# Who issues the rows of maxima: ScalarE's queue in place of SyncE's in two attention stages

## The reference

```
h = concatenate([x, latents], axis=1)                 # 256 + 256 tokens
q = (latents @ q_w + q_b).reshape(b, 256, 16, 16)     # 16 heads of width 16
kmat, v = the two halves of (h @ kv_w + kv_b)         # 512 keys
attn = einsum('bkhd,bnhd->bhkn', q, kmat) / 16
attn = where(full_mask, attn, -inf)
attn = softmax(attn)                                  # over the 512 keys
out = einsum('bhkn,bnhd->bkhd', attn, v) @ out_w + out_b + residual
out = rmsnorm(out); out = gelu(out @ mlp_w1 + mlp_b1) @ mlp_w2 + mlp_b2 + residual
```

## Time and profile before

| what | value |
|---|---|
| times, three runs | 1387.09, 1380.42, 1385.77 us, median 1385.77 |
| profiled execution | 1387.44 us, span 1385.6 us |
| PE busy | 1224.4 us (88%) |
| DVE busy | 991.2 us (72%) |
| ACT busy | 724.4 us (52%) |
| POOL busy | 496.1 us (36%) |
| granted clock of PE, mean over the span | 0.932 |
| DMA, mean over the span | 51 GB/s |
| exponential of a shifted score, line 1849 | 256 times, mean 605 ns, 132.1 us busy |
| row maxima, line 1864 | 128 times, mean 1211 ns, 151.9 us busy |
| two layers' rows of maxima, line 1827 | 64 DMAs of 2 KB |

### The profile page before, as it was taken

How to read it: one execution, slowest core, us unless ns; L and a number is a source line. 1 busy time by engine, 2 the same in 40 slices (tenths; PEclk the granted TensorE clock), 3 DMA queues, 4 the chain that set the end, 5 groups by cost and what they waited for, 6 DMA issues and landing times. The chain is left out here.

```text
span 1385.6 us, 27506 instructions
## 1 busy us (share of the span) xinstructions
PE 1224.4 (88%) x9162; PEld 1010.4 (73%) x9162; DVE 991.2 (72%) x2232; ACT 724.4 (52%) x1644; POOL 496.1 (36%) x649
## 2 busy tenths in 40 slices
PE   4799999999599999999599699969599976599969
PEld 4699999999599999998588455559377756455558
DVE  5688778887588887887773689465488866589464
ACT  3466656666366665666542177541166642177441
POOL 2754555444274445542150000030199950000030
PEclk8899999999899999999899789979799998699979
DMA  4111111010210111010013875020660014874020
GB/s 151 47 31 32 32 30 30 23 30 0 95 37 26 31 31 30 10 36 0 31 65 56 133 82 61 13 77 1 190 138 2 2 51 86 108 83 55 13 65 31
DMA packets 56609, 70.91 MB, mean 51 GB/s; under 512 B 7340, under 2 KB 49118, under 8 KB 54178
## 3 DMA queue, kind: packets, MB, share of 16 engines
q1 hardware_dynamic: 55420, 66.40, 22.7%
q10 hardware_dynamic: 1086, 3.20, 0.9%
HBM read 46.79 MB, written 8.13 MB: 40 GB/s over the span
## 5 line engine op out<-in xcount | busy, mean ns | idle before, releaser
L804 ACT ACTIVATE a_prob<-a_s_ps,a_negmax 128x257 f32<-128x257 f32 x256 | 119.2, 476 | 92.3 <-DVE a_negmax L894 92.3
L1864 DVE TENSOR_REDUCE s_mx<-s_s_ps 128x2 f32<-128x1024 f32 x128 | 151.9, 1211 | 17.8 <-PE s_s_ps L1909 17.6
L1849 ACT ACTIVATE s_probT<-s_st_ps 128x512 f32<-128x512 f32 x256 | 132.1, 605 | 59.9 <-PE s_st_ps L1923 57.5
L743 POOL TENSOR_TENSOR x_v_hi<-a_v_sum,x_one 128x512 fp32r<-128x512 f32 x60 | 63.2, 1054 | 242.5 <-DVE a_v_sum L883 242.4
L368 POOL MEMSET r_power<- 128x8 f32 x3 | 0.3, 105 | 362.7 <-POOLq L1976 329.3
L1653 POOL TENSOR_SCALAR s_below<-s_masked,s_mx 128x256 f32<-128x256 f32 x256 | 118.6, 485 | 27.9 <-DVE s_mx L1681 27.8
L909 DVE TENSOR_TENSOR a_pT_lo<-a_t_ps,a_pT_hi 128x512 fp32r<-128x512 f32 x128 | 88.2, 689 | 35.9 <-ACT a_pT_hi L817 34.2
L894 DVE TENSOR_REDUCE a_negmax<-a_s_ps 128x2 f32<-128x514 f32 x128 | 86.9, 688 | 26.0 <-PE a_s_ps L951 24.2
L1681 DVE CUSTOM_DVE_ANT_0 s_masked<-s_s_ps,l_mask 128x256 f32<-128x256 f32 x256 | 90.7, 421 | 15.5 <-PE s_s_ps L1718 15.5
L817 ACT ACTIVATE a_pT_hi<-a_t_ps 128x512 fp32r<-128x512 f32 x128 | 76.7, 600 | 47.3 <-PE a_t_ps L1005 44.1
L1666 ACT ACTIVATE s_probT<-s_st_ps 128x512 f32<-128x512 f32 x128 | 69.7, 595 | 28.3 <-PE s_st_ps L1728 28.3
(11 more groups left out here) (272 smaller groups left out, 4068.4 us busy)
## 6 DMA issues: line engine op xcount, KB each, us to landing
x_wqk_raw<-L_xattn_wq SPq DMA_DIRECT2D x32, 128.0 KB, 2.3
x_wqk_raw<-L_xattn_wk SPq DMA_DIRECT2D x32, 128.0 KB, 2.2
x_wv_raw<-L_xattn_wv SPq DMA_DIRECT2D x16, 256.0 KB, 3.1
a_wo_raw<-L_xattn_wo SPq DMA_DIRECT2D x16, 256.0 KB, 3.1
l_k_st<-k_second SPq DMA_DIRECT2D x12, 256.0 KB, 9.0
l_k_st<-k_stack SPq DMA_DIRECT2D x16, 192.0 KB
l_q_st<-q_stack SPq DMA_DIRECT2D x12, 192.0 KB
x_vbias<-L_xattn_bias_v SPq DMA_DIRECT2D x2, 1024.0 KB, 4.7
```

The costliest lines, as they stand in the source:

```text
L804: nc.scalar.activation(prob[:, n % 2, qt, 0:NK], s_ps[:, n % 2, qt, 0:NK], ACT.Exp, bias=negmax[:, n % 2, qt:qt + 1], accum_out=den[:, n % ...
L1849: nc.scalar.activation(probT[:, third % 2, n // 4, n // 2 % 2, n % 2], st_ps[:, u % 3], ACT.Exp, scale=c.scale).then_inc(z.exp_done, 1)
L1864: nc.vector.tensor_reduce(mx[:, i % 2, qt, a::2], s_ps[:, n % 2], AX.X, ALU.max).then_inc(z.max_done, 1)
```

## The change

The two row DMAs leave SP's stream and go to ACT's. ACT's order of a round gets a new step R0 between the third exponential (E2) and the fourth (E3); in it ACT waits for `mx_out` of the `second` quad and issues the two DMAs on its own queue. PE's, DVE's and POOL's streams stay as they were. SP's stream keeps all its loads, with no wait between those of different rounds but the one of line 1837.

```
-    act_steps = steps("E0 E1 E2 E3 E4 O0 E5 E6 E7")
+    act_steps = steps("E0 E1 E2 R0 E3 E4 O0 E5 E6 E7")
...
                 def body(first, second, third, fourth):
-                    if second is not None:
-                        g, b = batch(second)
-                        sp.wait_ge(z.mx_out, second + 1)
-                        for half in range(2):
-                            m = half * HALF + c.MAX_ROW
-                            sp.dma_start(slots[g % 3][0][m:m + 1, :, b].bitcast(F32),
-                                         mxT[2 * half:2 * half + 2, second % 2].bitcast(F32)
-                                         ).then_inc(row_in[second % 2], 16)
                     if first in (0, 1):
                         second_unit.load(c, sp, first == 0, slots[1][first == 0], unit_in[0])
...
+                        elif kind == "R" and second is not None:
+                            g, b = batch(second)
+                            act.wait_ge(z.mx_out, second + 1)
+                            for half in range(2):
+                                m = half * HALF + c.MAX_ROW
+                                act.dma_start(slots[g % 3][0][m:m + 1, :, b].bitcast(F32),
+                                              mxT[2 * half:2 * half + 2, second % 2].bitcast(F32)
+                                              ).then_inc(row_in[second % 2], 16)
```

## The result

The changed kernel takes 1417.91 us (median of 4 runs, 1416.81 to 1424.55) against 1386.19 us (4 runs): a ratio of 1.0247, 95% interval 1.0222 to 1.0272 (a ratio is worked out from all runs, not from the two medians, whose quotient is 1.0229). The forecast was 1381.8 us, its range 1374 to 1394. The profiled executions have spans of 1415.0 and 1385.6 us, so the traces show 29.4 us of it. The mean granted clock of TensorE is 0.922 after and 0.932 before.

A forecast was written before the change was run, and what follows sets the result against it. The start was taken to wait for data, the rest as a closed loop of the engines. Terms -9.1 + 2.0 + 0.7 + 1.6 + 0.8 = -4.0 us took 1385.8 to 1381.8 us, range 1374 to 1394.

The forecast's parts named there:

- Part 1: First row of each stage, layers 2 and 4: in its own queue it lands earlier, -9.1 us in all.
- one packet of the loads on the same engine: First row's landing: one 8.2 KB load packet gets in the way on a DMA engine, adding 1.0 us.
- 1.60 us: Estimated time from a row's issue to PE's release, taken from the second row with q1 nearly drained.
- Part 4: Traffic SP now sends at once: full-clock row waits +1.6 us, ACT's issues while SP issues +0.8 us.
- Part 2: Second row of each stage, issued while loads fill the engines: one packet more per layer, +2.0 us in all.
- Part 3: ACT's steady round: the issue pair's 1.02 us delay fits the 1.03 us slack; jitter costs +0.7 us.
- the table load: Exponential's table load, moved behind the first DMA pair: has 3.4 us before the first exponential, cost 0.
- rows at full clock: Part 4's row waits beside SP's loads: 0.2 us in each of 8 rounds, +1.6 us.
- issue beside SP: Part 4's cost of ACT issuing while SP issues: 0.1 us in each of 8 rounds, +0.8 us.
- Rival A: R0 at full clock beside group 3's loads: ACT pays for SP's traffic, +11 to +22 us, around 1400; chance 0.19.
- threshold of 1.85: Rival A's limit: an ACT issue pair above 1.85 us makes the change a loss.
- Rival B: Row late whichever queue, engines full: Parts 1 and 2 fall to 0, +3.1 us, 1388.9 us; chance 0.14.

The follow-up runs named there:

- c_kq: a_behind with group 1's key and query loads sent at once and only later loads paced, rows on ACT: 1397.95 us, ratio 1.008 to the kernel before.
- b_sp_last: Kernel before, rows still on SP but issued behind the loads of the round instead of ahead of them: 1395.88 us, ratio 1.0078.
- a_behind: Changed kernel with SP pacing its loads: round 1 waits for the first row's landing, later rounds for ACT's fourth exponential: 1390.19 us, ratio 1.0028.
- f_four: a_behind with four row DMAs of 1 KB per quad instead of two of 2 KB: 1439.46 us, ratio 1.0393 to the kernel before.
- a_mx: Changed kernel with SP again waiting for the same maxima ahead of the loads, rows still on ACT: 1387.53 us, ratio 1.0033 to the kernel before.
- d: Kernel before, rows on SP, loads spread: three key loads each in rounds 0 and 1, query loads in round 2, group 2 a round later: 1388.07 us, ratio 1.0019.
- h: Loads spread as in g, but on a_behind's ACT rows and SP waits: 1380.91 us, ratio 0.9985 to the kernel before.
- i: g with the constant rows behind the loads of round 2 instead of in round 0: 1385.06 us, ratio 0.9997 to the kernel before.
- g: Kernel before, rows on SP, loads spread finely over rounds 0 to 6, constant rows in round 0: 1379.42 us, ratio 0.9955; repeated 1378.18 us, 0.9951.
- j: g with all six query loads in round 2 and the constant rows in round 3 behind the loads: 1375.0 us, ratio 0.9935 to the kernel before.

## Why the prediction was wrong

**The bound.** It was read rightly: the start waits for data, the steady round is a closed loop with 1.03 us of slack for ACT. All but some 0.7 us of the loss falls in the start. One reading was too strict, that "a delay of O0 lengthens the round by as much": in the changed kernel rounds of 6.10 and 6.22 us in layer 2 are each followed by one of 5.7, so a single delay of 0.2 to 0.3 us is made good.

**Part 1 is the step that failed:** "After the change the row has a queue of its own", with a landing of "one packet of the loads on the same engine" behind its 1.60 us. Summed at -9.1 us, it came out at (9.94 - 4.92) + (11.17 - 5.76) = +10.4. Two things were wrong in it. The queue counts for little when the DMA engines have a backlog: c_kq and b_sp_last, and before and a_behind, agree within 0.9 us in both layers. And the backlog was taken as it stood before, 1.57 MB, when the change itself raises it to 2.56 (in layer 4 2.7). Even my end for the bad case, "a row that lands behind all 1.57 MB as before gives 0", held the bytes fixed. The wait for the maxima on SP was a wait for the row's data, but it was also what spaced the loads; I wrote down in Part 4 that SP "is never held by maxima any more", and did not bring that to Part 1.

**Part 2** counts one packet for the second row too: +2.0 us, measured 7.0 in layer 2 and 10.95 in layer 4, some 18, for the same reason with 4.3 and 4.7 MB ahead. So the two waits are 28 of the 29.4 us.

**Part 3** is right in its mechanism: +0.7 us forecast. From the first copy out to the thirteenth, layer 2 takes 70.79 us, before 70.68, and layer 4's 0.74 us more are the late row at 1275.80. The period is 5.90 us, the pair 1.17 us, the idle time ahead of the copy out nil. f_four shows the edge beside which the change stands. That the table load is hidden is right too: 1.28 us at 786.39, PE's first E at 798.

**Part 4** had the traffic in view but the wrong place for its price. "That the loads arrive earlier gains nothing" is true, and missed that they cost. Its rows at full clock (+1.6 us) met only the loads of group 3, since those of group 2 were all through by 814 us; one of them was late, by 0.66 us in layer 4. The issue beside SP (+0.8 us) cost PE 1.6 us once in layer 2 and 0.6 in layer 4 (a pair of 1.95 us at 1228.18), both at the low clock.

**Rival A** did not decide: pairs of 1.47 to 1.60 us beside the loads of group 3 (835.20 above) lengthen single rounds by 0.2 us (831.64 to 837.74, 6.10), which the next round gives back, and stay below its threshold of 1.85. Its mechanism is there, though, and where it bit hardest was the low clock: single issues of up to 2.41 us at 800.59 while SP's took 2.16 and 2.35.

**Rival B** had the right reason, "the row is late anyhow, because the engines are full, whichever queue it is in", a chance of 0.14, and a price of +3.1 us. That is about what a_mx (ratio 1.0033) and a_behind (1.0028) measure: B describes a change that keeps SP's pace. The real one needed a fourth case, B with the bytes that the removed wait lets through: (2.56 - 1.57) MB at 131 GB/s are 7.6 us at the first row, and (4.33 - 2.36) MB 15.0 us up to the second. Measured in layer 2 were 5.3 (798.08 against 792.78) and 15.2 (813.37 against 798.13). The first figure is too high, as in the table above. Two layers at 15 us are +30, a time near 1416 us. This is worked out afterwards, but the bytes and the rate were in front of me, and Part 4 itself had SP through with all these loads by about 800 us.

**The two rules** that I weighed. The Trainium skill, DMA: Bandwidth & Descriptors, "Issuing engines are not separate DMA queues", says that a second issuing engine saves only sequencer time. The measured delay agrees: the second issuer bought the row 0.2 to 0.9 us. The section also says that the DMAs of several engines interleave, which this row, behind a backlog, did not show. The other section, "Queues, rings and completion order", says that an engine goes round its queues packet by packet; by it four packets of ACT's queue should have moved soon after 786, and none moved before 795. The measurement decides: with this backlog the row kept the order of issue, to within 0.3 MB.

**Open:** where that order is kept. Bytes that an engine has already taken up, or one list for both queues in front of the engines, would look the same in these traces; packets in flight are seen when they move, not when they are taken. The rows that found little ahead of them fit either. No run issues the rows from a third engine, or from ACT with the loads on yet another queue. Nor is the loss of a_mx and a_behind wholly split. Counted from the first key load, their first copy out of layer 2 is at 29.03 and 29.97 us, 1.2 and 2.2 later than before (27.81), and that of layer 4 0.9 and 2.3 later; so a_mx loses 2.1 us at the two starts, of 2.5 to 6.6 by the timed runs. Its profiled span is all the same 0.8 us shorter than that of the kernel before, since its layer 2 stage begins 1.9 us earlier (775.49 against 777.43), by something ahead of the stage that was not looked into.

## What to carry to other kernels

A wait on an issuing engine does two jobs: it protects data, and it spaces all that the engine issues behind it. Before a small urgent transfer is moved to another queue, count the bytes that every queue will have issued ahead of it after the change, and divide by the rate that the windows show; if that sum grows, another queue doesn't help. It is an estimate: here it gave 7.6 us for the 5.3 measured at the first row, and 15.0 for 15.2 at the second. Where such a transfer is late, send fewer loads ahead of it, and look at which of the spread loads is late next: here three of five ways to spread them (d, h, i) brought no gain that the runs show, each with a new wait for a constant row or a query load, and two did (g by 0.5%, j by 0.65%).

## What the runs showed of the hardware

- A 2 KB transfer between SBUF places moved 10.4 us after its issue began (785.06 to 795.5), with 2.56 MB issued earlier by another engine, and ahead of loads that were issued later. Without other traffic (the pairs at 858.86 and 864.75 us) the packets of both DMAs moved 1.0 to 2.0 us after the pair's issue began.
- The issue of such a DMA takes ACT 0.566 us in the median, but 2.41 once while SP's issues took 2.16 and 2.35 us, with a backlog of about 1.4 MB (4.33 issued, 2.92 moved on q1 from 777 to 800.6). With twice as many issues (f_four) the median itself rose to 0.61 and 0.69 us.
- From the tenth copy out to the last, one layer took 36.1 us before (858.25 to 894.33) and 32.8 in b_sp_last, at the same work. The windows from 874 to 890 us, first the kernel before, then b_sp_last:

```profile
874.00:882.00 8.00, 8.00 (x83) 4.38 (x86) 3.86 (x6) 5.30 (x11) 0.00 (x0) 0.87 0.01 2
882.00:890.00 8.00, 8.00 (x62) 3.77 (x54) 0.50 (x2) 4.41 (x9) 0.00 (x0) 0.71 0.01 2
```

```profile
874.00:882.00 8.00, 8.00 (x86) 4.63 (x88) 7.45 (x11) 6.53 (x14) 0.00 (x0) 1.00 0.02 5
882.00:890.00 8.00, 7.93 (x84) 4.54 (x75) 3.32 (x7) 5.70 (x13) 0.00 (x0) 1.00 0.00 1
```

  PE is busy nearly throughout in both, but the granted clock is 0.87 and 0.71 in the one and 1.00 in the other. b_sp_last is some 7 us earlier in its work in these windows; its last rounds, from 886 to 894, are at 1.00 as well. A difference of 3 us in a single trace can come from there.
